# Second attention of a two-layer vision tower: softmax division moved from the probabilities to the values, row sums from ones columns in V

## The chip, the core and the metric

The kernel is one program on one core of a Trainium2 chip. Its time is the device time of one execution in microseconds (us). The core's engines each run their own queue in order: TensorE (PE; its weight loads are listed apart as PEld), VectorE (DVE), ScalarE (ACT), GpSimd (POOL) and SyncE (SP), which here only starts DMAs. They meet at semaphores alone.

## The reference

64 images of 64 tokens, 4096 tokens of width 256 in all. `h` goes through patch embedding, attention, a mixture of experts, a second attention and a second mixture of experts; each of the last four is added to `h` after a layernorm without weights. The second attention, the only part that is changed, has 16 heads of width 16:

```python
cq = gelu(x @ wq + bq);  ckv = gelu(x @ wkv + bkv)          # width 64
q = gelu(concat([cq @ wqc + bqc, rope(x @ wqr + bqr)]))     # 128 + 128
k = gelu(concat([ckv @ wkc + bkc, rope(x @ wkr + bkr)]))
v = ckv @ wv + bv
scores = einsum('bhqd,bhkd->bhqk', q, k) / sqrt(16)         # 64 x 64 per image and head, causal
attn = softmax(scores);  out = einsum('bhqk,bhkd->bhqd', attn, v)
return out @ wo + bo
```

## The kernel before

The stage `attention1_phase` runs over 8 tiles of 512 tokens (8 images), and each tile over 4 chunks of 128 tokens (2 images). Chunk number is g, its tile t, its place in the tile c. n is the next tile. Projections of tile n are made while tile n - 1 is in its attention. All order is written out by hand, in one function `pair` for each engine that lists calls of small helpers; the lists are unrolled in Python. Each helper waits for its inputs by a semaphore and counts another up.

For one chunk the way is: `scores` (TensorE, L2566; two masks as 128x512 products and 16 matmuls of a 32-row head pair, into the PSUM tile p_s, which is single) - `shift` (VectorE, L2403 to L2408: maximum per row, subtraction, into s) - `exp` (ScalarE, L2314, in place in s) - `row_sums` (VectorE, L2410 to L2414: sum per row, reciprocal) - `probabilities` (GpSimd, L2223: s times the inverse sum, 128 x 1024) - `turn_probabilities` (TensorE, L2590: eight 128x128 transposes into p_t) - `turned_out` (ScalarE, L2318: copy to pt) - `values` (TensorE, L2597 to L2605) - `output_high`, `output_low` (ScalarE L2322, VectorE L2416: the attention's output plus the bias of V, split into a rounded part ot_hi and the rest ot_lo) - `output` (TensorE, L2610: ot by wo, six matmuls, into columns 0 to 255 of p_w) - `add` (VectorE, L2424 to L2429: into h).

In `values` the weights are V: vz holds V of 8 head pairs, for each pair 32 columns, with one head's 64 keys in the upper and the other's in the lower partitions and zeros elsewhere. A matmul takes a 128 x 32 block of vz as weights and 64 queries of pt as the moving operand, and its result lands with the features on the partitions: 32 partitions by 64 queries. Four head pairs fill the four column groups of the array. The result is therefore already turned as `output` wants its weights. A 32-bit matmul shows as two records, so a chunk's 16 matmuls are x32 in the rows.

Beside the chunks, tile n needs `turn_rows`, `from_rows` 0 to 4 (the compressed part and the four rope products; each six 512-column matmuls), `from_compressed` (Q and K of the compressed part) and `values_in` 0 to 3 on TensorE, two banks of p_j in turn; `turned_high`, `compressed`, `queries_keys`, `values_out` on ScalarE, which also loads a table whenever it changes between gelu and exp; `turned_low`, `compressed_low`, `rotate` 0 to 3, `normalised`, `statistics` on VectorE; `rope_add` and `add_bias` on GpSimd. In tiles 0 and 1 GpSimd also gathers the last rows of the expert stage before (`late_gather`), and VectorE works them in, in `late_pieces`, in tile 2 (rows) and tile 3 (their statistics).

## Time and profile before

| | us |
|---|---|
| median of 3 runs (lowest, highest) | 1619.34 (1617.81, 1620.17) |
| span of the profiled execution, the only time the page gives for it | 1622.5 |
| PE busy in it, PEld busy | 1393.5 (86%), 1221.3 (75%) |
| DVE, ACT, POOL busy | 1051.8 (65%), 755.3 (47%), 643.1 (40%) |
| mean granted TensorE clock, of full speed | 0.927 |
| the second attention, from its first matmul to its last addition into h | 884.0 to 1189.7 |

A row of the windows view below gives for each engine its busy time and, in brackets, its number of instructions, then the TensorE clock granted, the DMA engines' busy share and the rate. A row of a timeline is: start, duration, engine, line, operation, output<-inputs, shape, count; brackets at its end hold the idle time of the engine ahead of it and what ended it. A matmul's duration includes its way through the array, so a row of many, one behind the other, ends later than the next group starts.

### The profile page before, as it was taken

The numbers are of one execution on the slowest core, as the hardware profiler recorded it, in microseconds if no ns is written. First come the engines' busy times: TensorE is split into PE (matmuls) and PEld (weight loads), VectorE is DVE, ScalarE is ACT, GpSimd is POOL, SyncE is SP. The second block draws the span as 40 slices with busy tenths as digits, with TensorE's granted clock in tenths as the row PEclk, the third lists the DMA queues.
The fourth block names the chain that finished last, engine by engine and source line by source line (L and its number), as shares of the span: only waits on it lengthen the run. The fifth ranks groups of instructions, "written<-read, shape, count | busy, mean of one in ns | idle before, by whom it ended". The sixth has DMA issues, their size and how long they took to land. (4 is left out here: it accounts for less than half of the span.)

```text
span 1622.5 us, 37180 instructions
## 1 busy us (share of the span) xinstructions
PE 1393.5 (86%) x14188; PEld 1221.3 (75%) x14188; DVE 1051.8 (65%) x2196; ACT 755.3 (47%) x1288; POOL 643.1 (40%) x720
## 2 busy tenths in 40 slices
PE   6979999999999986888881888899866999989983
PEld 5867878888888875888880566666666889989983
DVE  4754565575475487766665468988758857466754
ACT  5424444444444443244550567777632355645520
POOL 4015312102102004465445255343364565663665
PEclk9999999999999997889995899999956999999997
DMA  7314655235235005246762000000063377877843
GB/s 281 117 29 169 227 170 180 78 128 174 92 120 183 2 2 208 79 139 217 217 189 65 7 28 21 2 1 2 2 249 121 105 240 242 261 240 240 258 140 91
DMA packets 142884, 215.58 MB, mean 133 GB/s; under 512 B 14336, under 2 KB 112768, under 8 KB 141824
## 3 DMA queue, kind: packets, MB, share of 16 engines
q1 hardware_dynamic: 121648, 160.20, 29.9%
q0 software_dynamic: 18624, 52.45, 10.2%
q8 instruction: 119, 1.95, 0.5%
q10 hardware_dynamic: 2448, 0.61, 0.2%
q14 instruction: 45, 0.37, 0.1%
HBM read 103.64 MB, written 109.58 MB: 131 GB/s over the span
## 5 line engine op out<-in xcount | busy, mean ns | idle before, releaser
L125 PE MATMUL e_p_gu<-e_w_hi,e_xt_hi 128*128 (+1 forms) x676 | 202.4, 299 | 10.0 <-DVE e_xt_lo L723 9.5
L125 PE MATMUL e_p_gu<-e_w_hi,e_xt_lo 128*128 (+1 forms) x676 | 196.5, 291 | 0.0
L125 PE MATMUL e_p_gu<-e_w_lo,e_xt_hi 128*128 (+1 forms) x676 | 196.5, 291 | 0.0
L1273 POOL DMA_INDIRECT e_xn<-results,e_row_of x112 | 115.0, 1027 | 77.8 <-issue 42.4
L125 PEld LDWEIGHTS e_p_gu<-e_w_hi,e_xt_hi 128*128 128x128 f32 x676 | 134.5, 199 | 12.4 <-issue 12.0
L125 PEld LDWEIGHTS e_p_gu<-e_w_lo,e_xt_hi 128*128 128x128 f32 x676 | 134.9, 200 | 0.0
L125 PEld LDWEIGHTS e_p_gu<-e_w_hi,e_xt_lo 128*128 128x128 f32 x676 | 134.9, 199 | 0.0
L125 PE MATMUL e_p_y<-e_w_hi,e_hid_hi 128*128 (+1 forms) x338 | 112.6, 333 | 9.0 <-DVE e_hid_lo L742 7.0
L1254 POOL DMA_INDIRECT rows<-e_xn,e_row_of x96 | 94.2, 981 | 60.1 <-issue 41.8
L1940 DVE TENSOR_TENSOR a_ot_lo<-a_O,a_ot_hi 128x1024 fp32r<-128x1024 f32 x32 | 39.1, 1223 | 114.6 <-ACT a_ot_hi L1883 114.6
L125 PE MATMUL a_J<-a_xt_hi,w_qk_hi 128*128 128x512 f32 x256 | 106.9, 418 | 7.4 <-DVE a_xt_lo L1958 5.4
L2223 POOL TENSOR_TENSOR a_s<-a_s,a_total 128x1024 f32<-128x1024 f32 x32 | 60.9, 1904 | 118.2 <-DVE a_total L2414 117.5
L1299 ACT ACTIVATE e_gated<-e_p_gu 128x256 f32<-128x256 f32 x112 | 43.2, 385 | 126.0 <-PE e_p_gu L125 105.1
L125 PE MATMUL a_J<-a_xt_lo,w_qk_hi 128*128 128x512 f32 x256 | 101.3, 396 | 0.0
L125 PE MATMUL a_J<-a_xt_hi,w_qk_lo 128*128 128x512 f32 x256 | 101.3, 396 | 0.0
L125 PE MATMUL e_p_y<-e_w_lo,e_hid_hi 128*128 (+1 forms) x338 | 97.5, 288 | 0.0
L125 PE MATMUL e_p_y<-e_w_hi,e_hid_lo 128*128 (+1 forms) x338 | 97.3, 288 | 0.0
L1357 DVE TENSOR_TENSOR e_xt_lo<-e_p_xt,e_xt_hi 128x512 fp32r<-128x512 f32 x98 | 67.5, 689 | 23.5 <-ACT e_xt_hi L1292 15.5
L1292 ACT CAST e_xt_hi<-e_p_xt 128x512 fp32r<-128x512 f32 x98 | 57.5, 586 | 53.3 <-PE e_p_xt L1592 49.2
L1524 DVE SCALAR_TENSOR_TENSOR h<-e_xn,e_weight,h 128x256 f32<-128x256 f32 x112 | 54.2, 484 | 40.3 <-DMA e_xn<-results,e_row_of 37.3
L125 PE MATMUL a_J<-a_w_hi,a_ot_hi 128*128 128x256 f32 x256 | 73.5, 287 | 7.7 <-DVE a_ot_lo L1940 7.7
L1837 POOL CAST w_qk_in<-w_qk_in 128x768 fp32r<-128x768 f32 x24 | 21.9, 913 | 146.5 <-DMA w_qk_in<-in_we 146.5
(335 smaller groups left out, 4383.0 us busy)
## 6 DMA issues: line engine op xcount, KB each, us to landing
e_moved<-rows SPq DMA_DIRECT2D x121, 256.0 KB
results<-e_y SPq DMA_DIRECT2D x121, 256.0 KB
rows<-a_zero SPq DMA_DIRECT2D x28, 1024.0 KB, 5.8
pa_x<-in_x SPq DMA_DIRECT2D x7, 1536.0 KB, 6.4
w_qk_in<-in_we SPq DMA_DIRECT2D x24, 384.0 KB, 6.3
we_parts<-w_qk_in SPq DMA_DIRECT2D x24, 384.0 KB, 2.3
we_parts<-a_e_lo SPq DMA_DIRECT2D x24, 384.0 KB, 2.4
e_w_hi<-we_parts SPq DMA_DIRECT2D x4, 1536.0 KB, 16.1
```

Of the source, the lines that this page charges most:

```text
L125: mm = eng.matmul(out, lhs[a], rhs[b], start=start and n == 0, stop=stop and n == len(terms) - 1, skip_group_check=skip)
L1254: pool.indirect_dma_start(out=d["rows"][c][0:rooms[c] * P], out_offset=bass.IndirectOffsetOnAxis(ap=row_of[:, n, k:k + 1], axis=0), in_=ow ...
L1273: pool.indirect_dma_start(out=yg[g % RING][:, k, :], out_offset=None, in_=d["results"][c][0:rooms[c] * P], in_offset=bass.IndirectOffsetOn ...
L1292: act.copy(xt[0][i % 2][:], p_xt[i % 2][:]).then_inc(xt_hi, 1)
L1299: act.activation(gated[h % 2][:], p_gu[h % 2][:].rearrange("p (b n) -> p b n", n=2 * INNER)[:, :, 0:INNER], ACT.Silu)\
L1357: dve.tensor_tensor(xt[1][i % 2][:], p_xt[i % 2][:], xt[0][i % 2][:].bitcast(F32), ALU.subtract).then_inc(xt_lo, 1)
L1524: last = dve.scalar_tensor_tensor(row, yg[g % RING][:, k, :], weight[:, n, k:k + 1], row, ALU.mult, ALU.add)
L1837: pool.tensor_copy(e_hi, e_in).then_inc(e_split, 1)
L1940: dve.tensor_tensor(ot[1][:], p_o[:].rearrange("p i (j q) -> p j i q", q=SEQ), ot[0][:].bitcast(F32), ALU.subtract)\
L2223: pool.tensor_tensor(row_groups(s[c]), row_groups(s[c]), per_row(totals[c]), ALU.mult).then_inc(p_done, 1)
```

## The change

The probabilities are no longer divided. `exp` is followed by the transposes directly. vz gets two more columns for each head pair (V_COLS = 34), set to one once at the start, each in its head's partitions, so that the values product gives each row's sum beside the values. For that product the operands change places: a 128 x 64 block of pt is the weights, the 34 columns of vz move, and the result has the queries on the partitions: 64 partitions by 34 columns, two images in the two halves of the array. VectorE then takes the reciprocal of the 16 sums per token and multiplies the 256 values by it, out of PSUM into a new tile o (`scale`). TensorE turns o by two 128x128 transposes into the unused columns 256 to 511 of p_w (`turn_outputs`), from where `output_high` and `output_low` read. `row_sums` and `probabilities` go. The order of all four lists is rewritten: a chunk's output steps come later by a part of a slot, `output` now stands behind the scores of its slot, `exp(g + 3)` behind `values_out` 0 and 1, `rotate(n, 3)` behind `output_low(g)`, and `output_high(g + 2)` and `output_low(g + 2)` behind the splitting of the turned rows of tile n + 1.

The diff, blank lines and untouched lines left out where marked:

```diff
--- before.py
+++ after.py
@@ -44,6 +44,7 @@
...
+V_COLS = 2 * DK1 + 2
...
@@ -2165,10 +2166,11 @@
...
-        vz = [sb(f"vz{i}", [P, IMG_T, PAIRS, 2 * DK1]) for i in range(2)]
+        vz = [sb(f"vz{i}", [P, IMG_T, PAIRS, V_COLS]) for i in range(2)]
...
-        mx, totals = sb("mx", [P, 2 * PAIRS]), [sb(f"total{i}", [P, 2 * PAIRS]) for i in range(CH)]
+        mx, inv = sb("mx", [P, 2 * PAIRS]), sb("inv", [P, PAIRS, 2])
...
+        o = sb("o", [P, PAIRS, 2, DK1])
...
@@ -2184,10 +2186,13 @@
...
-        row_tile, max_done, s_out, exp_done, summed, inverse, p_done = (
-            sem(n) for n in ("row_tile", "max", "s_out", "exp", "summed", "inverse", "p_done"))
+        row_tile, max_done, s_out, exp_done, inverse, scaled, o_turned = (
+            sem(n) for n in ("row_tile", "max", "s_out", "exp", "inverse", "scaled", "o_turned"))
...
+
+        sums_and_values = p_o[:, 0:PAIRS * V_COLS].rearrange("p (j f) -> p j f", f=V_COLS)
+        p_ot = p_w[:, D:2 * D]
...
@@ -2207,6 +2212,11 @@
...
+            pool.wait_ge(zeros, 1)
+            for i, part in enumerate(vz):
+                for head in range(2):
+                    pool.memset(part[SEQ * head:SEQ * (head + 1), :, :, 2 * DK1 + head:2 * DK1 + head + 1], 1.0).then_inc(zeros, 1)
+                    pool.wait_ge(zeros, 2 + 2 * i + head)
...
             def add_bias(t):
@@ -2217,11 +2227,6 @@
...
-            def probabilities(g, c):
-
-                pool.wait_ge(inverse, g + 1)
-                pool.tensor_tensor(row_groups(s[c]), row_groups(s[c]), per_row(totals[c]), ALU.mult).then_inc(p_done, 1)
-
             def rope_add(n, i, place):
...
@@ -2237,10 +2242,8 @@
             def pair(t2, last=False):
...
-                    g = CH * t
...
-                    probabilities(g + 1, 1)
...
@@ -2249,22 +2252,16 @@
                         rope_add(t + 1, 2, K_SWAP)
...
-                    probabilities(g + 2, 2)
-                    if few is not None:
...
-                    probabilities(g + 3, 3)
-                    if few is not None:
...
-                        probabilities(g + 4, 0)
...
-            probabilities(0, 0)
...
@@ -2321,10 +2318,10 @@
             def output_high(g):
-                act.wait_ge(o_mm, g + 1)
+                act.wait_ge(o_turned, g + 1)
...
-                    done = act.activation(ot[0][:, b], p_o[:, b * P:(b + 1) * P], ACT.Identity, bias=bias[:, 7 + b:8 + b])
+                    done = act.activation(ot[0][:, b], p_ot[:, b * P:(b + 1) * P], ACT.Identity, bias=bias[:, 7 + b:8 + b])
...
             def pair(t2, last=False):
@@ -2333,31 +2330,32 @@
...
                     turned_out(g)
+                    if not is_first(t):
+                        output_high(g - 1)
...
+                    exp(g + 2, 2)
+
+                    turned_out(g + 1)
...
-                    exp(g + 2, 2)
-
-                    turned_out(g + 1)
...
                         queries_keys(n, 1 - u)
+
+                    turned_out(g + 2)
...
-
-                    exp(g + 3, 3)
...
                         values_out(n, 1 - u, range(0, 2))
-                    turned_out(g + 2)
+                    exp(g + 3, 3)
...
                         values_out(n, 1 - u, range(2, 4))
                         exp(g + 4, 0)
...
-                    output_high(g + 2)
-
+
+                    turned_out(g + 3)
...
                         turned_high(n + 1)
-                    turned_out(g + 3)
-                    output_high(g + 3)
+                    output_high(g + 2)
...
                         exp(g + 5, 1)
...
@@ -2368,7 +2366,7 @@
...
             queries_keys(0, 0)
-            act.wait_ge(zeros, 1)
+            act.wait_ge(zeros, 5)
             values_out(0, 0, range(4))
             exp(0, 0)
             turned_high(1)
@@ -2376,6 +2374,7 @@
...
+            output_high(CH * TILES - 1)
...
         def _(dve):
@@ -2407,16 +2406,20 @@
...
-            def row_sums(g, c):
-                dve.wait_ge(exp_done, g + 1)
-                dve.tensor_reduce(totals[c][:], row_groups(s[c]), AX.X, ALU.add).then_inc(summed, 1)
-                dve.wait_ge(summed, g + 1)
-                dve.reciprocal(totals[c][:], totals[c][:]).then_inc(inverse, 1)
+            def scale(g):
+
+                dve.wait_ge(o_mm, g + 1)
+                dve.reciprocal(inv[:], sums_and_values[:, :, 2 * DK1:V_COLS]).then_inc(inverse, 1)
+                dve.wait_ge(inverse, g + 1)
+                at_least(dve, o_turned, g)
+                dve.tensor_tensor(o[:], sums_and_values[:, :, 0:2 * DK1].rearrange("p j (h f) -> p j h f", f=DK1),
+                                  inv[:].rearrange("p j (h f) -> p j h f", f=1).broadcast_to([P, PAIRS, 2, DK1]),
+                                  ALU.mult).then_inc(scaled, 1)
             def output_low(g):
...
-                    done = dve.scalar_tensor_tensor(ot[1][:, b], p_o[:, b * P:(b + 1) * P], bias[:, 7 + b:8 + b],
+                    done = dve.scalar_tensor_tensor(ot[1][:, b], p_ot[:, b * P:(b + 1) * P], bias[:, 7 + b:8 + b],
...
@@ -2441,52 +2444,54 @@
...
-                    row_sums(g + 1, 1)
...
-                        add(t - 1, g - 1, 3)
+                        output_low(g - 1)
                     shift(g + 2, 2)
...
                         rotate(n, 0)
-                    output_low(g)
+                    if not is_first(t):
+                        add(t - 1, g - 1, 3)
...
+                    scale(g)
...
                         rotate(n, 1)
                         rotate(n, 2)
+
+                    output_low(g)
+                    if more:
                         rotate(n, 3)
-
-                    row_sums(g + 2, 2)
+                    shift(g + 3, 3)
                     add(t, g, 0)
-                    shift(g + 3, 3)
-                    output_low(g + 1)
+                    scale(g + 1)
...
                         normalised(n + 1)
...
-                    add(t, g + 1, 1)
-                    row_sums(g + 3, 3)
+                    output_low(g + 1)
...
                         shift(g + 4, 0)
+                    add(t, g + 1, 1)
...
+                    scale(g + 2)
...
                         statistics(t - 1)
-                    output_low(g + 2)
...
                         turned_low(n + 1)
+                    output_low(g + 2)
...
-                        row_sums(g + 4, 0)
                         shift(g + 5, 1)
                     add(t, g + 2, 2)
-                    output_low(g + 3)
+                    scale(g + 3)
...
@@ -2521,12 +2526,12 @@
                 rotate(0, i)
             shift(0, 0)
             turned_low(1)
-            row_sums(0, 0)
             shift(1, 1)
...
+            output_low(CH * TILES - 1)
...
@@ -2588,7 +2593,7 @@
...
             def turn_probabilities(g, c):
-                pe.wait_ge(p_done, g + 1)
+                pe.wait_ge(exp_done, g + 1)
...
@@ -2598,14 +2603,24 @@
...
+                at_least(pe, scaled, g)
...
-                    for i in range(2):
-                        for q in range(4):
-                            mm = pe.matmul(p_o[32 * q:32 * q + 32, b * P + i * SEQ:b * P + (i + 1) * SEQ],
-                                           vz[u][:, 2 * c + i, 4 * b + q, :], pt[:, scored(b, q), i * SEQ:(i + 1) * SEQ],
+                    for q in range(4):
+                        for i in range(2):
+                            mm = pe.matmul(p_o[SEQ * i:SEQ * (i + 1), (4 * b + q) * V_COLS:(4 * b + q + 1) * V_COLS],
+                                           pt[:, scored(b, q), i * SEQ:(i + 1) * SEQ], vz[u][:, 2 * c + i, 4 * b + q, :],
...
+
+            def turn_outputs(g):
+
+                pe.wait_ge(scaled, g + 1)
+                at_least(pe, ot_lo, g)
+                rows = o[:].rearrange("p j h f -> p (j h f)")
+                for b in range(KD):
+                    mm = pe.transpose(p_ot[:, b * P:(b + 1) * P], rows[:, b * P:(b + 1) * P], core.ident[:])
+                mm.then_inc(o_turned, 1)
             def output(g):
...
@@ -2622,35 +2637,41 @@
...
                     turn_probabilities(g, 0)
...
-                        output(g - 1)
+                        turn_outputs(g - 1)
                     scores(t, u, g + 2, 2)
...
                         from_rows(n, 1)
+                    if not is_first(t):
+                        output(g - 1)
                     values(t, u, g, 0)
...
                         from_rows(n, 2)
                         from_rows(n, 3)
                     turn_probabilities(g + 1, 1)
-                    output(g)
+                    turn_outputs(g)
...
                         from_rows(n, 4)
...
                     scores(t, u, g + 3, 3)
+                    output(g)
                     values(t, u, g + 1, 1)
                     turn_probabilities(g + 2, 2)
...
                         values_in(n, range(0, 2))
+                    turn_outputs(g + 1)
+                    if more:
+                        scores(n, 1 - u, g + 4, 0)
                     output(g + 1)
...
-                        scores(n, 1 - u, g + 4, 0)
                         values_in(n, range(2, 4))
                     values(t, u, g + 2, 2)
                     turn_probabilities(g + 3, 3)
...
+                    turn_outputs(g + 2)
...
                         scores(n, 1 - u, g + 5, 1)
                     output(g + 2)
@@ -2669,6 +2690,7 @@
             from_rows(1, 0)
...
+            turn_outputs(CH * TILES - 1)
             output(CH * TILES - 1)
```

## Rows read from the trace of the kernel before

**Rows 1.** Windows view, one row per tile: engine busy, count, clock.

```profile
918.10:956.70 38.60, 35.15 (x383) 26.34 (x383) 24.28 (x35) 25.06 (x37) 20.76 (x16) 0.83 0.10 29
956.70:993.20 36.50, 31.02 (x390) 23.28 (x389) 29.37 (x48) 24.85 (x37) 20.72 (x16) 1.00 0.10 30
...
1028.80:1064.40 35.60, 29.85 (x385) 22.46 (x385) 32.06 (x71) 24.59 (x37) 12.50 (x7) 1.00 0.01 2
...
1096.70:1129.10 32.40, 30.55 (x390) 23.03 (x390) 26.91 (x48) 24.90 (x38) 12.56 (x8) 1.00 0.01 2
1129.10:1160.00 30.90, 29.00 (x379) 21.58 (x377) 24.38 (x43) 23.34 (x35) 12.51 (x8) 1.00 0.01 2
1160.00:1190.00 30.00, 20.44 (x270) 15.74 (x258) 19.72 (x43) 11.42 (x19) 7.58 (x5) 0.73 0.01 1
```

**Rows 2.** Who waited for GpSimd's multiplication L2223: us in total, times.

```profile
  PE a_T L2593: 19.9, 17
```

**Rows 3.** Groups by line, 985 to 1154 us: busy us, mean ns, idle before.

```profile
L2223 POOL TENSOR_TENSOR a_s<-a_s,a_total 128x1024 f32<-128x1024 f32 x21 | 40.0, 1904 | 72.9 <-DVE a_total L2414 72.3
...
L2412 DVE TENSOR_REDUCE a_total<-a_s 128x16 f32<-128x1024 f32 x20 | 24.3, 1213 | 1.6 <-ACT a_s L2316 1.3
...
L2429 DVE TENSOR_TENSOR h<-h,a_W 128x256 f32<-128x256 f32 x20 | 7.7, 387 | 1.2 <-PE a_W L125 1.1
...
L2414 DVE RECIPROCAL a_total<-a_total 128x16 f32<-128x16 f32 x20 | 5.1, 253 | 0.7
```

**Rows 4.** Timeline of TensorE's weight loads in tile 5.

```profile
1101.30 0.44 PEld L2586 LDWEIGHTS a_S<-a_kz,a_qt 32*64 32x64 f32 x16 [0.42 <-issue]
...
1104.29 0.49 PEld L2605 LDWEIGHTS a_O<-a_pt,a_vz 128*32 128x32 f32 x32 [0.36 <-issue]
```

**Rows 5.** Timeline of TensorE's matmuls in tile 5.

```profile
1101.30 1.46 PE L2586 MATMUL a_S<-a_kz,a_qt 32*64 32x128 f32 x32
...
1104.29 0.65 PE L2605 MATMUL a_O<-a_pt,a_vz 128*32 128x64 f32 x32
...
1107.74 1.03 PE L2593 MATMUL a_T<-ident,a_s 128*128 128x128 f32 x8
...
1111.72 0.50 PE L125 MATMUL a_J<-a_comp_hi,w_attention_hi 128*128 128x512 f32 x1 [0.17 <-DVE a_rope L2397]
...
1118.13 0.36 PE L125 MATMUL a_W<-w_attention_hi,a_ot_hi 128*128 128x256 f32 x1 [0.28 <-DVE a_ot_lo L2419]
...
1118.92 0.60 PE L2578 MATMUL a_S<-mask_bf,ident_bf 128*128 128x512 bf16 x2
...
1123.30 1.09 PE L2593 MATMUL a_T<-ident,a_s 128*128 128x128 f32 x8 [0.17 <-POOL a_s L2223]
...
1127.02 0.38 PE L125 MATMUL a_W<-w_attention_hi,a_ot_hi 128*128 128x256 f32 x1
```

**Rows 6.** Timeline of ScalarE in tile 5.

```profile
1108.81 1.01 ACT L2320 COPY a_pt<-a_T 128x1024 f32<-128x1024 f32 x1 [0.80 <-PE a_T L2593]
...
1117.36 1.28 ACT L2316 ACT_TABLE_LOAD   x1
1118.66 1.06 ACT L2316 ACTIVATE a_s<-a_s 128x1024 f32<-128x1024 f32 x1
1119.62 1.50 ACT L2310 COPY a_vz<-a_J 64x256 f32<-64x256 f32 x4
...
1124.71 0.63 ACT L2327 ACTIVATE a_ot_hi<-a_O,a_bias 128x128 fp32r<-128x128 f32 x2
1125.30 1.01 ACT L2278 CAST a_xt_hi<-a_J 128x1024 fp32r<-128x1024 f32 x1
```

**Rows 7.** Timeline of VectorE in tile 5.

```profile
1110.91 0.75 DVE L2397 SCALAR_TENSOR_TENSOR a_rope<-a_J,a_bias,a_sin 128x512 f32<-128x512 f32 x1 [1.98 <-PE a_J L125]
...
1125.51 0.60 DVE L2419 SCALAR_TENSOR_TENSOR a_ot_lo<-a_O,a_bias,a_ot_hi 128x128 fp32r<-128x128 f32 x2
1126.34 1.23 DVE L2385 TENSOR_TENSOR a_xt_lo<-a_J,a_xt_hi 128x1024 fp32r<-128x1024 f32 x1 [0.23 <-ACT a_xt_hi L2278]
```

2 lines of the change are left out of this document (1 added, 1 removed).

## The prediction

> **What bounds the kernel now.** Only the second attention is changed, so I read first the windows of that stage, one for each tile of 512 tokens [rows 1]. Tiles run 30.9 to 38.6 us. In tile 5 (1096.7 to 1129.1) TensorE is busy 30.55 us of 32.40, VectorE 26.91, ScalarE 24.90, GpSimd 12.56: TensorE is the bound with under 2 us left. In tile 3 (1028.8) TensorE does 29.85 of 35.60 and VectorE 32.06: it carries late pieces there (in tile 2 the rows of the combine before, in tile 3 their statistics), and both engines wait in turn. Two tiles have no row of their own: tile 2 lasts the 35.6 us of tile 3, tile 4 the 32.3 of tile 5. Then who stops TensorE: the GpSimd multiplication by the inverse sums. The transposes of the probabilities waited for it 19.9 us in 17 places [rows 2], which is nearly all of what TensorE loses. Last, the engines' order inside a tile [rows 4 to 7]: there one sees which work lies between a chunk's steps, and that has to be redone for the new order.
>
> **What the change removes.** Per chunk (32 of them): a VectorE sum of 1.21 us and a reciprocal of 0.25, and the GpSimd multiplication of 1.90 [rows 3]. The way from the exponential to the transposes gets 3.4 us shorter, so all 19.9 us of those waits should go: exp(g+1) is finished long before its transposes in every slot. From VectorE's load comes back the new reciprocal (same size, 0.25, taken from PSUM) and the multiplication of 128x256 out of PSUM, for which the nearest row is the addition of the same size, 0.39 us [rows 3]. VectorE gets 1.46 - 0.64 = 0.8 us less per chunk, 3.3 per tile. Nothing of that is on TensorE's path in tiles 4 and 5.
>
> **What it adds on TensorE.** First two transposes per chunk. Eight take 1.03 us with their tail [rows 5], so two are bounded by a quarter of it, 0.26, and by half, 0.5, since a group has a fill and a tail however short it is; I take 0.3, nearer to the first, because the next group starts before the tail is out. Second, the values product. Now its 32 weight loads are 32 columns wide, in four column groups, and take 0.49 us, the group 0.65 [rows 4, 5]. New, the probabilities are the weights: 64 columns each, in two groups, with 34 columns moving in place of 64. Bound below: as now, 0.65. Bound above: the scores' 32 matmuls, with 64 columns loaded and 128 moving, take 1.46 us [rows 5]. Nearest are the scores' loads, also 64 wide: 16 in 0.44 us [rows 4], so 32 in 0.88; doubled width in half the groups makes 0.49 into 0.98. I take 1.05 for the group, +0.4. Sum on TensorE: 0.7 us per chunk, 2.8 per tile, 22 in all. That is already about the 20 us given back.
>
> Two rules weighed beside this. By the Trainium skill, page "TensorE: Matmul & The Clock Gate", section "LDWEIGHTS (loading the stationary operand)", a load takes its columns divided by 1.2 GHz: 27 ns for 32 columns, 53 for 64. In a row of 32 this would be 0.85 us now; the trace has 0.49, so loads of different column groups overlap here, and the doubling stands. By the page "TensorEngine Tiling (Array Packing)", section "Instruction Overhead", a matmul with few moving columns is no shorter than one with about 60: going from 64 to 34 would give nothing back; no row of before shows a moving operand that narrow.
>
> **Where new waits come.** I wrote the new order of all four queues out with the rows' durations. Two places give way.
> (a) Last slot, TensorE's output(g+2). In the old order ot_hi of that chunk came ahead of ScalarE's xt_hi, and ot_lo ahead of xt_lo. Now, from the moment that turn_outputs(g+1) is done, ScalarE does one after another ot_hi 0.63, V copies 1.50, the table load 1.28, exp 1.06, V copies 1.50, exp 1.06, pt 1.01, xt_hi 1.01 [rows 6] = 9.05; then VectorE xt_lo 1.23 and ot_lo 0.60 [rows 7], together 10.9, with pick-ups 11.1. TensorE has between the same points: from the scores at 1118.92 to output at 1127.02 8.10 us, plus output(g+1) 0.79 (1118.13 to 1118.92), which moved in there, plus 0.7 of new work, less 0.17 old idle [rows 5] = 9.4. Wait: 1.7 us. Queued behind it are values(g+3) and the next tile's first product, so it is on the path.
> (b) rotate 3 of the rope now stands behind output_low(g) on VectorE, which waits for ot_hi(g), which ScalarE makes after pt(g+1). From the transposes at 1107.74: pt is done 2.1 us later (1108.81 + 1.01), then ot_hi 0.63, ot_lo 0.60, rotate 0.75, 4.1 in all. TensorE was ready for the K product, which needs that bank, at 1111.55 (1111.72 less its 0.17 of idle): 3.8 us, less the output product of 0.79 that moved behind it, plus 0.3 of turn_outputs = 3.3. Wait 0.8 to 0.9 in place of the 0.17 of now [rows 5 to 7].
> The other new waits (scaled(g+1) ahead of turn_outputs) have cover: VectorE has the product's end and 0.9 us of its own, TensorE the eight transposes and, in every slot but the last, projections. add(g) now stands ahead of scale(g+1), but output(g) precedes values(g+1) on TensorE, so nothing is turned round.
>
> Edits at nothing: the four memsets of ones fall in the stage's opening, where GpSimd then waits for constants and for the rope anyway; the gathers of the late rows, no longer between multiplications, start sooner and are needed in tile 2 only; SP's queue is not touched. If the cover of the memsets were gone they would cost under 0.5 us once.
>
> **Sum.** A whole tile in the new order: 30.55 + 2.8 + 2.6 = 36.0 if every wait is added; written out queue by queue the order closes at 35.5, since busy time in the windows counts the tails of groups that a wait then covers. I take 35.5 (estimate from rows 1 and 5 to 7). Against now: tile 1 36.5 to 35.5, -1.0; tiles 2 and 3 have VectorE's late pieces, which stand in front of ot_lo in (a) (1.2 us more each): 36.7 against 35.6, +1.1 and +1.0; tiles 4 and 5 +3.1 each; tile 6 has no next-next tile to turn, so (a) is 0.9: +1.1. Tile 0 wins its first waits for GpSimd, a part of the 19.9, and pays (a) and (b): 0. The last tile is a chain, chunk by chunk: 1.21 + 0.25 + 1.90 = 3.4 us out and 0.25 + 0.39 + 0.3 of transposes, 0.4 of product and their pick-ups in, but its outputs wait for one another through ScalarE as in (a), and part of it ran at the lower clock [rows 1]: a gain of 1 us at most, taken as 0. Sum +8.4 us. The profiled execution spans 1622.5 us, 3.2 above the median of the runs (1619.3) and 2.3 above the highest of them, so a profile of the new kernel would be near 1631 and the median 1619.3 + 8.4 = 1627.7. Stages behind this one start at a barrier and take the shift whole.
>
> **The rivals.**
> 1. Faster: no new stall. If ScalarE's queue in (a) is ahead of my order by 1.5 us, because copies start sooner than I drew them, and the values product stays at 0.65 to 0.75, each tile is what TensorE needs: 30.55 + 4 x 0.3 = 31.8. Tile 1 gains 4.7, tiles 2 and 3 3.8 each, 4 and 5 0.5 each: -13, so 1606 to 1609. It decides at a stall under about 0.5 us per tile. For it speaks that VectorE and GpSimd lose load and that 19.9 us are real. Against it the ScalarE chain, whose every step is a row [rows 6]. Chance 0.22.
> 2. Even: product at 0.7 in place of 1.05, 1.4 us per tile, of which (a) takes 0.3 back; with seven tiles 7.7 less: 1620. Chance 0.16.
> 3. Loads and streams of the values product in series: 1.4 us (near the upper bound above), +0.35 on 32 chunks = 11, of which (a) hides a quarter: +8.4, 1636. Against it: the loads of now overlap, 32 of them in 0.49 us [rows 4]. Chance 0.13. (By the Trainium skill's rule above, loads in a row would make 32 x 53 ns = 1.7 us of it and some 1642 of the time.)
> 4. Clock. In the last stretch the granted clock is 0.73 and in tile 0 0.83 while tiles 1 to 6 hold 1.00 [rows 1]; 1.7 us of wait per tile, beside 0.9, could let it fall to 1.2 GHz within each tile. Tile 3 is idle for 5.75 us of its 35.6 and keeps 1.00, which speaks against. Tile 0 is the price: 38.6 at 0.83 against 35.5 is 3 us; in six tiles 18: 1645. Chance 0.09.
> Forecast itself 0.40.
>
> **How the numbers follow.** A measurement of this kernel tells about 0.2% (3.2 us). Faster by more: rival 1 and little else, 0.23. Within: rival 2 and the near edge of the forecast, 0.17. Slower: 0.60. The likeliest case has 1622 to 1634 for itself; the range goes to 1607, the faster rival, and to 1640, past rival 3, and leaves the clock case out.
>
> **What would show it.** Right: in tiles 4 and 5, 35 to 36 us each; TensorE waiting for ot_lo over 1 us once a tile; no wait of a_T for GpSimd; the values group about 1.0 us. Wrong: a tile of under 32.4 us there, a_W waiting nowhere over 0.5 us, or a values group of 0.65. Tile 1 should be faster in every case but the last two.

## The result, and the profile after

| | before | changed |
|---|---|---|
| median us (lowest, highest), 4 runs each | 1618.57 (1616.62, 1620.17) | 1643.22 (1637.72, 1648.49) |
| ratio, with its 95% interval | | 1.0134 (1.0104 to 1.0164) |
| profiled execution: span, and its own time | 1622.5 | 1646.7, 1648.49 |
| mean granted TensorE clock in it | 0.927 | 0.921 |
| PE, DVE, ACT, POOL busy | 1393.5, 1051.8, 755.3, 643.1 | 1416.7, 1026.0, 761.6, 581.5 |
| second attention, its first matmul to the next stage's first | 306.1 | 330.9 |

The changed kernel is 1.3% slower. The prediction said slower, by 8 us; it is 24.6 by the medians and 24.8 in the stage, so the loss is all in the stage that was changed, and the time lies outside the range. The busy times hold what the change moves: VectorE and GpSimd have 26 and 62 us less, TensorE 23 us more, by records that include what a lower clock adds.

The windows of the changed kernel, one row per tile as in [rows 1], cut in both kernels at the first transpose of a tile's chunk 0; columns: window, length, each engine's busy time and instructions, granted TensorE clock of full speed, DMA share, GB/s. First row: the opening, ahead of tile 0; last row: tile 7.

```profile
886.10:920.90 34.80, 24.62 (x150) 18.35 (x151) 17.23 (x16) 14.12 (x21) 11.82 (x11) 0.79 0.06 14
920.90:958.00 37.10, 34.12 (x386) 27.20 (x389) 21.84 (x36) 25.32 (x36) 13.05 (x11) 0.92 0.10 30
958.00:993.00 35.00, 32.29 (x393) 26.11 (x396) 23.97 (x47) 24.90 (x37) 11.03 (x9) 1.00 0.09 24
993.00:1031.60 38.60, 35.05 (x394) 28.18 (x397) 30.01 (x63) 24.90 (x37) 4.90 (x3) 0.93 0.01 1
1031.60:1071.60 40.00, 36.61 (x394) 29.77 (x397) 27.87 (x66) 26.40 (x39) 4.90 (x3) 0.88 0.01 1
1071.60:1110.20 38.60, 35.88 (x394) 29.13 (x397) 24.35 (x48) 24.90 (x37) 4.88 (x3) 0.90 0.01 1
1110.20:1148.50 38.30, 35.58 (x394) 28.88 (x397) 24.05 (x47) 24.90 (x37) 4.88 (x3) 0.90 0.01 2
1148.50:1181.50 33.00, 30.86 (x380) 25.02 (x382) 20.95 (x40) 23.42 (x36) 4.88 (x3) 0.97 0.01 1
1181.50:1217.00 35.50, 27.88 (x268) 22.97 (x269) 16.64 (x44) 10.95 (x19) 0.04 (x1) 0.60 0.00 1
```

For the comparison, the last tile of before in the same cut:

```profile
1161.90:1190.00 28.10, 20.29 (x258) 15.74 (x258) 17.85 (x42) 10.79 (x17) 5.71 (x4) 0.71 0.01 1
```

In that cut the tiles of before are 36.1 (opening), 38.5, 36.5, 35.6, 35.7, 32.3, 32.3, 30.9, 28.1. The changed kernel's, from the opening on, differ by -1.3, -1.4, -1.5, +3.0, +4.3, +6.3, +6.0, +2.1, +7.4: 24.9 us. Two things are to be seen. Tiles 4 and 5 were to take 35 to 36 us and take 38.6 and 38.3, with TensorE busy 35.9 and 35.6 of that. So they aren't idle; their matmuls last longer, and the clock column says why: 0.88 to 0.93 in tiles 2 to 5, where [rows 1] have 1.00, and 0.60 in the last tile against 0.71.

Whom TensorE waits for in this stage (engine, tile and line, then who ended it: us in total, times, longest):

```profile
PE a_W L126 <- DVE a_ot_lo L2422: 17.7, 12, 2.2
...
PE a_J L126 <- DVE a_rope L2396: 4.6, 10, 0.8
```

All 19.9 us of [rows 2] are gone, as drawn. In their place stand 17.7 for ot_lo (7.3 before) and 4.6 for the rope (2.9 before). With 0.8 for pt before and 1.4 for the scaled o after, these waits fell from 30.9 us to 23.7, and the stage lost 25: the length of the waits by itself can't be the reason.

Tile 4 of the changed kernel on TensorE (start, duration, engine, line, operation, tiles, shape, count; in brackets the idle time ahead and what ended it):

```profile
1085.81 0.51 PE L126 MATMUL a_J<-a_comp_hi,w_attention_hi 128*128 128x512 f32 x1 [0.63 <-DVE a_rope L2396]
...
1097.37 1.13 PE L2611 MATMUL a_O<-a_vz,a_pt 128*64 128x34 f32 x32
...
1100.32 0.38 PE L2622 MATMUL a_W<-ident,a_o 128*128 128x128 f32 x2
...
1104.23 0.36 PE L126 MATMUL a_W<-w_attention_hi,a_ot_hi 128*128 128x256 f32 x1 [1.70 <-DVE a_ot_lo L2422]
...
1105.24 0.41 PE L126 MATMUL a_W<-w_attention_hi,a_ot_lo 128*128 128x256 f32 x1
1105.59 1.93 PE L2611 MATMUL a_O<-a_vz,a_pt 128*64 128x34 f32 x32
1107.45 0.79 PE L126 MATMUL a_J<-a_xt_hi,w_attention_hi 128*128 128x512 f32 x1
```

The wait ahead of output(g+2), (a) of the prediction, is 1.70 us, where 1.7 was drawn. The rows around it have the rest of the loss. Ahead of it a values product takes 1.13 us; behind it the very same 32 matmuls take 1.93, the output product's matmuls go from 0.28 to 0.41, and the projections of 512 columns from 0.39 and 0.50 to 0.63 and 0.79. That is the engine at the lower of its two levels, 1.2 GHz in place of 2.4. It stays so until 1112, some 7 us. The other waits for ot_lo have the same behind them: 2.20 us at 1025.67, then half speed to 1033; 1.10 at 1056.28, for 3.4 us; 0.97 at 1066.10, to 1074; 1.70 at 1142.33, to 1149; 1.12 at 1178.73, to 1193; and in the last tile 1.46, 1.94 and 1.55, with half speed from 1200 to its end. Behind 1.70 at 953.03 it lasts 3.4 us, and behind 1.70 at 989.60 there is none. That last one ends tile 1, which holds 1.00 and lasts 35.0 us: the change with its wait but without the fall, half a microsecond under the forecast's whole tile.

By the windows, (1 - clock) times twice the length is the time at half speed: 81 us in this stage against 44 before (14.6 + 5.9 + 0 + 5.4 + 9.6 + 7.7 + 7.7 + 2.0 + 28.4 for the rows above). 37 us more at half speed are at most 18.5 us of delay. With it the loss reads up to 18.5 for the clock and 6 or more for what the prediction had in its sum.

### The profile page after: what moved, and what is told of

It is laid out like the page before. It is cut to its first block and busy times, and to the rows that moved or that the text cites. A ratio compares the mean times of both kernels' runs of the same rounds, so it can differ in the third digit from the quotient of the medians.

```text
span 1646.7 us, 37296 instructions
## 1 busy us (share of the span) xinstructions
PE 1416.7 (86%) x14221; PEld 1253.0 (76%) x14252; DVE 1026.0 (62%) x2196; ACT 761.6 (46%) x1288; POOL 581.5 (35%) x692
## 5 line engine op out<-in xcount | busy, mean ns | idle before, releaser
L1255 POOL DMA_INDIRECT rows<-e_xn,e_row_of x96 | 94.6, 985 | 57.3 <-POOL router_bias L1249 35.7
L2233 POOL TENSOR_TENSOR a_rope<-a_rope 128x512 f32<-128x512 f32 x16 | 20.5, 1281 | 214.5 <-DVE a_rope L2396 214.5
L126 PEld LDWEIGHTS e_p_y<-e_w_hi,e_hid_hi 128*128 128x128 f32 x338 | 66.2, 196 | 10.6 <-DVE e_hid_lo L743 7.1
```

The lines of the kernel that those rows point to most:

```text
L126: mm = eng.matmul(out, lhs[a], rhs[b], start=start and n == 0, stop=stop and n == len(terms) - 1, skip_group_check=skip)
L1255: pool.indirect_dma_start(out=d["rows"][c][0:rooms[c] * P], out_offset=bass.IndirectOffsetOnAxis(ap=row_of[:, n, k:k + 1], axis=0), in_=ow ...
L2233: pool.tensor_tensor(rope[i][:], rope[i][:], rope[i + 1][:], ALU.add).then_inc(rope_sum, 1)
```

## The experiments

Two theories stood after that. The clock theory (C in the expectations): the work and the waits that the change adds are worth what the forecast says, about 8 us, and the other 17 come from the clock, which falls behind wait (a). Its rival (W): the waits and the added work take all of it themselves, through the order of the queues, and the clock is only a companion. In the kernels below that carry added products, these read constants and write to free columns that nobody reads afterwards; nothing of the computation is left out. The kernel before was run again beside each group of experiments, median 1621.91 us (31 runs) for e1 to e4, 1620.89 (29) for e5 to e8, 1622.18 (22) for e9 and e10; each ratio is to those. The kernel before ran from 1613 to 1632 in them, wider than in the first four runs, so ratios and their intervals are compared, not times across groups.

### The wait shortened by order: e1_splits_first

The ScalarE chain of (a) has xt_hi 1.02 ahead of ot_hi and, on VectorE, xt_lo 1.22 ahead of ot_lo. Both are put behind, as in the kernel before:

```diff
                     turned_out(g + 3)
+                    output_high(g + 2)
                     if not last:
                         turned_high(n + 1)
-                    output_high(g + 2)
...
+                    output_low(g + 2)
                     if not last:
                         turned_low(n + 1)
-                    output_low(g + 2)
```

> The changed kernel with one thing turned back: in a tile's last slot ScalarE makes ot_hi(g+2) ahead of xt_hi, and VectorE ot_lo(g+2) ahead of xt_lo, as in the kernel before. This takes away wait (a) of the prediction (1.70 us in a whole tile of the changed kernel) and leaves all added TensorE work. Theory C (the wait is what lets the clock fall: after each of these waits the records run at half speed for some 7 us): the half-speed stretches inside tiles 2 to 6 go too, and the kernel gains 1.7 us for the wait and some 3.5 us for the clock in each of five or six tiles, so 1643 becomes about 1618 to 1623, granted clock 1.00 in the tiles. Rival W (the clock falls for the stage's mixture of work, whatever the waits): the wait alone goes, 6 x 1.7 = 10 us, 1633, and half-speed stretches stay in the tiles.

Measured: 1624.37 us (1618.01 to 1628.64), 1.0019 (0.9992 to 1.0046). Tiles 1, 2, 5 and the last:

```profile
954.40:988.40 34.00, 32.51 (x393) 26.09 (x396) 24.09 (x48) 24.77 (x37) 11.04 (x9) 1.00 0.09 25
988.40:1025.40 37.00, 34.27 (x394) 27.51 (x397) 30.32 (x65) 25.81 (x38) 4.90 (x3) 0.95 0.01 2
1094.20:1128.20 34.00, 32.50 (x393) 26.08 (x396) 24.12 (x48) 24.77 (x37) 4.88 (x3) 1.00 0.01 1
1160.70:1189.20 28.50, 20.33 (x270) 16.00 (x268) 17.02 (x46) 11.12 (x19) 0.01 (x1) 0.87 0.00 1
```

Two swapped pairs take nearly all of the loss back, 1.0134 to 1.0019; the median is 1.4 us above the 1618 to 1623 that theory C gave and 9 below W's 1633. Where the wait is gone the tile holds 1.00 and lasts 34.0. In tile 2 a wait of 1.06 us is left ahead of the same output product (late pieces on VectorE), and behind it the values product takes 1.88 us and the clock of the tile is 0.95: 37.0. This kernel alone doesn't tell C from W, since it removes wait and fall together.

### The wait kept, but filled: e2_filled_wait

Here the order of the changed kernel is left as it is, and so is ot_lo's time. TensorE is given something to do while it waits:

```diff
                         scores(n, 1 - u, g + 5, 1)
+                    if not last:
+                        for _ in range(12):
+                            pe.matmul(p_o[:, 272:512], core.ident_bf[:], core.mask_bf[:, 0:240], start=True, stop=True)
                     output(g + 2)
```

> The changed kernel with its wait (a) kept but filled: ahead of output(g+2) TensorE does twelve 128x240 bf16 products of the mask into columns of the values' bank that nobody reads, 1.2 us of the 1.7, in each tile that turns rows. The chain over ScalarE and VectorE is untouched, so a tile's dependencies are as long as before. Theory C: TensorE is never idle for long, the clock stays at 1.00 within the tiles, and the time falls by the clock's share alone, 3.5 us in five or six tiles: 1623 to 1628. Rival W: no change, 1643, or a little slower.

Measured: 1625.56 us (1620.33 to 1631.51), 1.0024 (1.0004 to 1.0043). The wait of tile 4, with the twelve products ahead of it:

```profile
1096.31 1.40 PE L2679 MATMUL a_O<-mask_bf,ident_bf 128*128 128x240 bf16 x12
1098.08 0.36 PE L126 MATMUL a_W<-w_attention_hi,a_ot_hi 128*128 128x256 f32 x1 [0.36 <-DVE a_ot_lo L2422]
```

Tiles 1, 2, 5 and the last:

```profile
959.40:994.40 35.00, 33.62 (x405) 27.20 (x408) 23.95 (x47) 24.89 (x37) 11.02 (x9) 1.00 0.09 24
994.40:1030.40 36.00, 33.82 (x405) 27.25 (x408) 28.52 (x60) 24.89 (x37) 4.90 (x3) 1.00 0.01 2
1101.50:1136.50 35.00, 33.63 (x405) 27.22 (x408) 23.96 (x47) 24.89 (x37) 4.88 (x3) 1.00 0.01 1
1168.50:1200.00 31.50, 23.53 (x270) 18.90 (x269) 17.11 (x46) 11.12 (x19) 0.03 (x1) 0.73 0.00 1
```

This is what decides. Nothing of the real work got shorter, TensorE got more to do, and the kernel is 1.1% faster than the changed one: 17.7 us by the medians. The clock is 1.00 in tiles 1 to 6, and their lengths are 35.0, 36.0, 36.1, 35.0, 35.0 and 32.0: against before -1.5, +0.4, +0.4, +2.7, +2.7, +1.1, which is the forecast's tile list (-1.0, +1.1, +1.0, +3.1, +3.1, +1.1) within 0.7 us each. Tile 1 lasts the 35.0 us that it had in the changed kernel, where it held 1.00 too: the fillers themselves changed nothing in it. W fell. The last tile has no filler and keeps 0.73, +3.4 against before.

### The added work alone: e3_before_more_pe

The kernel before, with TensorE made busier by 0.87 us per chunk (eight products of 256 columns) ahead of each values product, 28 us of work in all. The change has 0.92 per chunk by its profile (the values product from 0.58 to 1.06 and turn_outputs 0.44, start to start), where the forecast had 0.7. No wait is added.

```diff
                 hold(pe, pt_out, g + 1)
+                for _ in range(8):
+                    pe.matmul(p_o[:, 0:256], core.ident_bf[:], core.mask_bf[:, 0:256], start=True, stop=True)
                 for b in range(KD):
```

> The kernel before with TensorE work added and nothing else: eight 128x256 bf16 products of the mask ahead of each values product, 0.87 us per chunk, what the changed kernel added there by its profile (values 0.58 to 1.06, turn_outputs 0.44 from start to start). Their result is overwritten. If the added work is the larger part of the loss (28 us of work, minus what old idle time hides, 6 us in tiles 1 to 3): 1618 becomes 1636 to 1642 and the clock stays. If added work costs less because TensorE waited anyway: below 1630.

Measured: 1623.7 us (1620.34 to 1628.38), 1.0019 (1.0001 to 1.0037). Tile 0, tile 4, and the last:

```profile
918.00:953.70 35.70, 33.40 (x410) 25.80 (x414) 24.27 (x35) 24.94 (x37) 20.69 (x15) 0.97 0.11 31
1063.00:1097.00 34.00, 33.21 (x417) 25.67 (x420) 27.20 (x49) 26.33 (x39) 12.51 (x7) 1.00 0.01 2
1162.90:1188.50 25.60, 18.52 (x288) 14.16 (x291) 17.72 (x42) 11.25 (x19) 5.74 (x4) 1.00 0.00 1
```

Of the two cases of the expectation the second came, work that costs little (below 1630), and not 1636 to 1642: 3 us by the ratio. In tiles 4 and 5, with under 2 us of idle time in them, 3.5 us of work cost 1.7. In tile 0 and in the last tile the filled time brought more than it cost: the clock goes from 0.85 to 0.97 and from 0.71 to 1.00, and the tiles from 38.5 to 35.7 and 28.1 to 25.6. TensorE waited 8.5 us for GpSimd in place of 19.9. The 3 us are therefore a sum: what the work costs (0.4 to 1.7 us in each of tiles 1 to 6, all at 1.00), less what the clock gives back, since the half-speed time of the stage falls from 44 us to about 20, at most 12 us of gain. This profile is the quickest of its ten executions. The prediction's "22 in all. That is already about the 20 us given back" set work against waits at full price.

### The order alone, in the old kernel: e4_before_late_splits

The kernel before, with only the order of the last slot taken from the change: xt_hi ahead of ot_hi, xt_lo ahead of ot_lo.

```diff
-                    output_high(g + 2)
-
                     if not last:
                         turned_high(n + 1)
+                    output_high(g + 2)
...
-                    output_low(g + 2)
                     if t >= 2:
                         next(late_pieces, None)
...
                     if not last:
                         turned_low(n + 1)
+                    output_low(g + 2)
```

> The kernel before with only the order of the last slot changed as in the changed kernel: ScalarE makes xt_hi ahead of ot_hi(g+2), VectorE xt_lo ahead of ot_lo(g+2). Theory C: a wait of 0.5 to 1 us per tile comes in front of output(g+2), 3 to 6 us in all, and where it is long enough the clock falls for 7 us: 1622 to 1635, with half-speed stretches inside tiles that had none. Rival W: the wait alone, 1621 to 1624, clock 1.00 in tiles 1 to 6.

Measured: 1625.77 us (1624.22 to 1631.07), 1.0022 (1.0005 to 1.0039). Tiles 1, 2, 3 and 5:

```profile
959.70:998.60 38.90, 33.08 (x386) 26.11 (x389) 29.98 (x48) 25.20 (x38) 20.70 (x15) 0.88 0.10 28
998.60:1036.30 37.70, 33.05 (x385) 25.52 (x388) 31.78 (x62) 24.85 (x37) 12.51 (x7) 0.91 0.01 2
1036.30:1073.50 37.20, 32.26 (x385) 24.64 (x387) 30.36 (x65) 23.79 (x36) 12.52 (x7) 0.94 0.01 2
1106.40:1140.40 34.00, 31.63 (x385) 24.31 (x390) 27.95 (x51) 25.57 (x38) 12.52 (x7) 0.95 0.01 1
```

And the wait of tile 1 on TensorE, with a row from behind it:

```profile
993.31 0.55 PE L125 MATMUL a_W<-w_attention_hi,a_ot_hi 128*128 128x256 f32 x1 [2.72 <-DVE a_ot_lo L2418]
...
994.08 0.41 PE L125 MATMUL a_W<-w_attention_hi,a_ot_hi 128*128 128x256 f32 x1
```

The wait for ot_lo is 2.72 us in tile 1, 1.88 in tile 2 (at 1031.03, also followed by a row of 0.55), 0.69 in tile 3 and 1.14 in tiles 4 and 5. The first row behind the wait has 0.55 and a later one 0.41 where [rows 5] have 0.36 for the first; half speed lasts to 1000 behind the one and to 1037.5 behind the other, and of the two of 1.14 us the one in tile 5 has 3.4 us behind it and the one in tile 4 none. So a wait in this place drops the clock without anything of the change. Not all of the lower clock in tiles 1 and 3 is of this kind: 3.4 us of it in each stand behind waits for GpSimd of 2.43 us (at 978.06) and 2.07 (at 1064.09). The loss is only 3.6 us by the ratio, and that time alone would fit both theories; only the trace tells. The profiled execution, 1630.93 us, is the second slowest of the ten, so the usual one may have fewer falls than these rows. In this kernel there is no extra TensorE work, and the transposes that follow wait for GpSimd anyway; that part of the slow stretch falls on idle time would explain the small sum, and wasn't tested by itself.

### The changed kernel again: e8_changed_again

The changed kernel unaltered, on the chip on which e5 to e7 ran.

> The changed kernel as it is, so that the others of this call stand beside it on the same chip. Both theories: 1.2 to 1.6% over the kernel before, half-speed stretches after most of the waits for ot_lo in the last slots.

Measured: 1646.72 us (1634.67 to 1658.14, 6 runs), 1.0132 (1.0097 to 1.0166). The ratio repeats. The tiles of its profile differ: tile 1 lasts 38.6 at 0.90 here and 35.0 at 1.00 in the first, tile 5 38.1. In this execution, the slowest of its six, every wait for ot_lo of 0.96 us and more in tiles 0 to 6 has half speed behind it, also the one of 1.70 at the end of tile 1. So which waits are followed by a fall isn't the same from one execution to the next; the run times spread over 23 us, those of the filled kernel over 11.

### The other wait: e5_rotate_first

e1, and on top rotate 3 back ahead of output_low(g), which should take away wait (b):

```diff
                         rotate(n, 2)
+                        rotate(n, 3)

                     output_low(g)
-                    if more:
-                        rotate(n, 3)
```

> The kernel with the splits of chunk g+2 first (as in e1) and, besides, rotate(n, 3) ahead of output_low(g) on VectorE, which is wait (b) of the prediction undone: 0.63 us in each of seven tiles in the profiles of the changed kernel and of e1. If (b) is on the path: tiles of 33.4 us where e1 had 34.0, 3 to 4 us in all. If something else is late right behind it (ot_lo(g), then output(g)): tiles stay at 34.0 and the time at e1's, 1.002 of before.

Measured: 1623.53 us (1618.69 to 1625.86), 1.0006 (0.9989 to 1.0023). Tile 4 and the last:

```profile
1060.70:1094.30 33.60, 32.87 (x393) 26.06 (x396) 23.84 (x49) 26.26 (x39) 4.90 (x3) 1.00 0.01 2
1159.90:1191.40 31.50, 23.54 (x271) 18.91 (x269) 17.15 (x47) 11.12 (x19) 0.07 (x1) 0.74 0.00 1
```

The waits for a_rope in the stage fall from 4.3 us (e1) to 1.4, and tiles 4 and 5 from 34.0 to 33.6, expected 33.4: 0.4 for a wait of 0.63. In all, 3 to 4 us were expected; the ratios of e1 and e5 differ by 2, with intervals that overlap. The last tile is at 0.74, 31.5 us against 28.5 at 0.87 in e1, though nothing in it was edited; the two profiles differ there by the clock alone. Against the changed kernel on the same chip, 1646.72, the orders undone together are worth 23 us, of the 26 that it is above the kernel before there.

### Fillers where the clock fell: e6_repaired_filled and e7_before_filled

e6 is e5 with fillers where its trace still had the lower clock: in the opening, in tile 6 and in the last tile, whose outputs wait for one another. e7 gives the kernel before the same opening and its own last tile's fillers.

```diff
+            def fill(out, count):
+                n = out.shape[-1]
+                for _ in range(count):
+                    pe.matmul(out, core.ident_bf[:], core.mask_bf[:, 0:n], start=True, stop=True)
...
+                    if not more:
+                        fill(p_j[:, 0, :], 6)
                     output(g + 1)
...
+                    if not more:
+                        fill(p_j[:, 0, :], 9)
+                    elif last:
+                        fill(p_o[:, 272:512], 8)
                     output(g + 2)
...
             turn_rows(0)
+            fill(p_o[:], 8)
...
             from_compressed(0)
+            fill(p_o[:], 12)
             values_in(0, range(4))
             scores(0, 0, 0, 0)
             turn_rows(1)
+            fill(p_o[:], 6)
             scores(0, 0, 1, 1)
+            fill(p_o[:], 5)
...
+            fill(p_j[:, 0, :], 3)
             turn_outputs(CH * TILES - 1)
+            fill(p_j[:, 0, :], 7)
             output(CH * TILES - 1)
```

e7 has the four fills of the opening, 4 more ahead of the first transposes, and in the last tile 2 ahead of the transposes of g+2, 3 ahead of output(g+1), 12 ahead of the transposes of g+3 and 7 ahead of the last output.

> e5 plus fillers: mask products in bf16 of 512 or 240 columns that nobody reads, put where TensorE stands idle in the stage's opening (8, 12, 6 and 5 of them), in the slot before the last tile and in the last tile (8, 6, 9, 3, 7). Theory C: the clock stays at full speed in tile 0 and up to the end of the stage, which had 14 half-speed us in e1 beyond the opening; 3 to 7 us less than e5 and the runs scatter less: 0.995 to 0.998 of before. Rival: fillers only cost their own time where they outlast a wait, 0 to 3 us more than e5.

> The kernel before with the same fillers in the opening (and 4 ahead of the first transposes) and 2, 3, 12 and 7 of them ahead of the waits of its last tile: the control for e6. Theory C: its 27 half-speed us in tile 0 and the last tile fall to under 10, 5 to 9 us less: 0.994 to 0.997 of before. The difference of e6 to this one is then the change's own worth with the clock held in both: more TensorE work, 1.1 us per tile in tiles 4 and 5, less waiting in tiles 1 to 3; about even.

e6 measured: 1616.07 us (1609.93 to 1620.03), 0.9963 (0.9946 to 0.998). Tile 2 and the last:

```profile
986.80:1023.70 36.90, 34.28 (x394) 27.42 (x397) 30.29 (x65) 25.84 (x38) 4.90 (x3) 0.95 0.01 2
1157.80:1184.80 27.00, 23.94 (x292) 16.84 (x293) 17.02 (x46) 11.13 (x19) 0.00 (x0) 1.00 0.01 1
```

e7 measured: 1620.88 us (1616.24 to 1624.98), 0.9995 (0.9978 to 1.0012). Tiles 1, 3 and the last:

```profile
955.30:993.90 38.60, 33.70 (x385) 26.57 (x390) 29.28 (x48) 24.95 (x37) 20.68 (x15) 0.87 0.10 29
1029.40:1067.60 38.20, 33.25 (x384) 24.66 (x388) 32.39 (x71) 24.79 (x37) 12.52 (x7) 0.91 0.01 2
1163.20:1190.90 27.70, 23.36 (x278) 16.54 (x283) 17.90 (x43) 10.79 (x17) 5.76 (x4) 0.82 0.00 1
```

e6 is the first kernel that is faster than before. The last tile goes from 31.5 at 0.74 (e5) to 27.0 at 1.00 with 25 more products in it, whose rows have 5.4 us together. Tile 2 still has its fall, 36.9 at 0.95. The runs were to scatter less than e5's and did not: 10 us against 7. e7 missed: 0.994 to 0.997 was expected of it. The opening and the last tile did gain, but tiles 1 and 3, untouched by the fillers, fell to 0.87 and 0.91: tile 1 behind a wait for GpSimd of 2.44 us (1.22 in the profile of before) and one for ot_lo of 1.53, tile 3 behind one for GpSimd of 1.72. In the profile of before, waits of 1.63 for ot_lo and 1.74 for GpSimd in the same places went by at 1.00. So the step from e7 to e6 isn't a clean price of the change with the clock held; that price stays open.

### How long the wait must be: e9_part_filled

e2 with six fillers in place of twelve, so that a part of (a) is left:

```diff
+                    if not last:
+                        for _ in range(6):
+                            pe.matmul(p_o[:, 272:512], core.ident_bf[:], core.mask_bf[:, 0:240], start=True, stop=True)
                     output(g + 2)
```

> The dose: as e2, but six fillers of 240 columns in place of twelve, so that of the 1.70 us of wait (a) some 1.1 is left. If any wait of over 1 us lets the clock fall: half-speed stretches in the tiles nearly as in the changed kernel, 1.009 to 1.013 of before. If what counts is how long TensorE stands in one go and 1.1 us is short enough (the kernel before has waits of 1.2 to 2.1 us in tiles 1 to 3, mostly without a fall): as e2, 1.001 to 1.004.

Measured: 1633.06 us (1625.76 to 1638.87), 1.0057 (1.0033 to 1.0081); its profiled execution took 1630.81. Tiles 3 and 5, and the wait that is left in tile 4:

```profile
1028.90:1066.80 37.90, 35.48 (x403) 28.61 (x402) 28.03 (x67) 24.96 (x38) 4.90 (x3) 0.94 0.01 2
1101.90:1137.00 35.10, 33.33 (x404) 26.67 (x403) 23.95 (x47) 24.90 (x37) 4.88 (x3) 1.00 0.01 1
```

```profile
1098.45 0.36 PE L126 MATMUL a_W<-w_attention_hi,a_ot_hi 128*128 128x256 f32 x1 [0.98 <-DVE a_ot_lo L2422]
```

The time is between the two expectations. 1.70 us of wait: 1.0132 and 1.0134; 0.98 left: 1.0057; under 0.4 left in tiles 1, 4 and 5 (e2): 1.0024. In the profile, of the fifth quickest of twelve executions, 0.98 us went by at 1.00 in tiles 1, 4 and 5, while tile 3, behind 1.47 at the end of tile 2 and with 1.08 of its own, fell to 0.94. The runs are graded with the length of the wait, not cut at one length; the way that fits both is that a wait drops the clock in some executions and some tiles, and the more often the longer it is. The kept traces bear that out as far as they go. Of the waits for ot_lo in tiles 0 to 6, those of 1.70 us (four each in the two profiles of the changed kernel) have half speed behind them in 7 cases of 8, both of 2.2 us too. Those of 0.96 to 1.13 us have it in 6 of 6 cases in these two profiles, and in 3 of 17 in the profiles of e1, e2, e5, e6, e9 and e10, where the waits of 1.70 us are shortened or gone. So the length isn't all of it.

### Fillers in tiles 2 and 3 as well: e10_filled_late_tiles

e6 plus fillers in tiles 2 and 3, one slot ahead, where the late pieces make TensorE wait:

```diff
                     if not more:
                         fill(p_j[:, 0, :], 6)
+                    elif t in (2, 3):
+                        fill(p_o[:, 272:512], 9)
                     output(g + 1)
```

> e6 with nine more fillers of 240 columns ahead of output(g+1) in tiles 2 and 3, where VectorE's late pieces hold ot_lo back by 1.1 us and where e6 still had one half-speed stretch of 3.4 us. If that stretch comes from this wait: 0 to 2 us less than e6, 0.995 to 0.997 of before, and nothing at half speed between the opening and the end of the stage. If not: as e6.

Measured: 1613.89 us (1611.1 to 1623.22), 0.995 (0.9932 to 0.9968). Tiles 0, 2 and the last:

```profile
922.90:956.80 33.90, 31.72 (x390) 25.04 (x389) 21.02 (x33) 24.24 (x35) 13.05 (x11) 1.00 0.12 33
990.30:1026.00 35.70, 33.85 (x407) 26.99 (x406) 28.89 (x61) 24.91 (x38) 4.91 (x3) 1.00 0.01 2
1160.10:1187.20 27.10, 24.25 (x298) 16.88 (x294) 17.05 (x47) 11.12 (x19) 0.06 (x1) 1.00 0.00 1
```

Its profiled execution, 1623.22 us, is the slowest of its twelve; the time above the others isn't in this stage: against e6's profile the stage starts 3.4 us later, is 1.0 shorter and has 4.6 us more behind it. Every tile holds 1.00, and they last 33.9, 33.5, 35.7, 34.9, 33.6, 33.6, 32.0 and 27.1, the stage 297.0 us against 306.1 before. It beats the kernel before by 0.5% and the changed one by 1.8%; from e6 it isn't told apart, their intervals overlap. Its tiles 4 and 5 are still 1.3 us longer than [rows 1]; it wins in the opening, in tiles 0, 1 and 3 and in the last.

## Why the prediction missed

**What held.** The reading of the bound (TensorE, waits for GpSimd of 19.9 us), and that all of them go. The values product: 1.05 was taken, from the width of its weight loads; 1.13 was measured for the group and 1.06 from its start to the next group's, the weight loads 1.01 against 0.49 in [rows 4]. With that rival 3, which needed 1.4, is out, and rival 2, which needed 0.7, too. By the Trainium skill, page "TensorE: Matmul & The Clock Gate", section "LDWEIGHTS (loading the stationary operand)", 32 loads of 64 columns in a row are 1.7 us, as an estimate from its formula. The trace has 1.01 and speaks against, as [rows 4] did. Two rows of the changed kernel's stretch from 985 to 1154 us (group, count, busy us, mean ns, idle before):

```profile
L2611 PE MATMUL a_O<-a_vz,a_pt 128*64 128x34 f32 x546 | 22.6, 243 | 0.0
...
L2415 DVE TENSOR_TENSOR a_o<-a_O,a_inv 128x256 f32<-128x256 f32 x17 | 7.2, 424 | 0.6
```

The multiplication out of PSUM was put at 0.39 us by its size, 0.42 measured; the reciprocal at 0.25, 0.26 measured. Rival 1 fell at (a): ScalarE wasn't ahead of the order drawn. Its queue in tile 4, to be laid beside [rows 6]:

```profile
1095.37 1.28 ACT L2313 ACT_TABLE_LOAD   x1
1096.66 1.06 ACT L2313 ACTIVATE a_s<-a_s 128x1024 f32<-128x1024 f32 x1
...
1100.39 1.01 ACT L2317 COPY a_pt<-a_T 128x1024 f32<-128x1024 f32 x1
1101.30 1.02 ACT L2275 CAST a_xt_hi<-a_J 128x1024 fp32r<-128x1024 f32 x1
1102.20 0.64 ACT L2324 ACTIVATE a_ot_hi<-a_W,a_bias 128x128 fp32r<-128x128 f32 x2
```

The table load takes 1.28, exp 1.06, pt 1.01, xt_hi 1.02, ot_hi 0.64; then on VectorE xt_lo 1.22 from 1102.35 and ot_lo 0.60 from 1103.49: each step is there, in the order and the length of the working, and the wait comes out at 1.70.

**What was off in size.** turn_outputs 0.38, with 0.44 from its start to the next, where 0.3 was taken; wait (b) 0.63, where 0.8 to 0.9 was. A whole tile with the clock held is 35.0 us (e2), 35.5 in the forecast, and the tile list of the forecast is that of e2 within 0.7 us. That its sum came out is in part luck, as said below. What was wrong by more is the last tile, "a gain of 1 us at most, taken as 0": it is +7.4. In e10 the same chain at full clock is 27.1, which is -1.0 against the 28.1 of before at 0.71; so some 8 us of the 35.5 are the clock, which the 1.12 us at the end of tile 6 and the three waits of 1.46 to 1.94 us let fall. (Against e3's last tile, 25.6 at 1.00 without the change, 27.1 is 1.5 more; part of the old tile's time was clock as well.)

**The step that failed** is rival 4, its chance of 0.09 and the range that "leaves the clock case out". Its mechanism and place were right: 1.7 us of wait per tile and a fall to 1.2 GHz within the tile. Its price of 3 us was taken from tile 0 of the old kernel against a tile of the new one, and the total of 1645 (1643.2 measured) is near in part by luck: against e2 the profile has 2.6, 3.9, 3.6, 3.3 and 1.0 us in tiles 2 to 6, 14.4 in place of 18 in six tiles, nothing in tile 1, and 4.0 in the last tile, which the rival did not count. It was set aside by one sentence: "Tile 3 is idle for 5.75 us of its 35.6 and keeps 1.00, which speaks against". That is a sum over a tile, of many short waits, and says nothing on one wait of 1.7 us between two dense stretches. A row that could have spoken was in the same profile, where the last tile follows tile 6, 29.0 us busy of 30.9 at 1.00:

```profile
1161.92 1.09 PE L2593 MATMUL a_T<-ident,a_s 128*128 128x128 f32 x8 [1.77 <-POOL a_s L2223]
...
1164.48 1.08 PE L2578 MATMUL a_S<-mask_bf,ident_bf 128*128 128x512 bf16 x2
```

One wait of 1.77 us, and the masks behind it take 1.08 in place of the 0.60 of [rows 5]; half speed lasts from 1163 to 1170. The trace of before also holds waits of 1.63 and 2.06 us with no fall behind them, so it could not have given certainty; but a case that one row bears out and others speak against belongs inside the range.

**Two errors of size that cancelled.** The forecast's tile has 2.8 us of added work, 0.9 for (b) and 1.7 for (a), 5.4 in all, of which 1.85 of old idle time and 0.5 of cover are taken off: +3.1. Measured, with the clock at 1.00, the terms are 3.7 (0.92 per chunk), 0.6 and 1.7, 6.0 in all, and the tile is +2.7. So the work was put too low, and what hides behind other work too low as well; that the tile list came out is luck in part. By the experiments tiles 4 and 5 last 32.3 us before, 33.6 with the added work and hardly a wait for the rope (e5), 34.0 with wait (b) (e1) and 35.0 with wait (a) as well, filled (e2): 1.3 for 3.7 us of work, 0.4 for (b), 1.0 for (a). e3 has 1.7 for 3.5 us of other work. What covers the rest of the work, and whether a tile is as long as ScalarE's chain and its wait, no run separates.

**What stays open.** What decides whether a wait drops the clock: 1.70 us at 989.60 and those of 1.63 and 2.06 us before had no fall behind them, while 1.06 and 1.12 us had one in some places and none in others. Waits for the rope of 1.70 and 1.69 us in tile 0 of e6 and e10 had none either. And e1 was expected about 5 us ahead of e2; 1.2 was measured, with intervals that overlap. e1's profiled execution, 1620.78 us, is the second quickest of its ten and e2's, 1631.03, the second slowest, so the tiles of 34.0 may be e1's best and not its usual ones. What the change is worth with the clock held in both kernels is open too, since e7 did not hold it.

## What to carry to other kernels

A new wait on a busy TensorE costs up to its length and then what the lower clock makes of the work behind it: here 1.7 us of wait cost 1.0 by themselves, and were in most cases followed by 3.4 to 7 us of matmuls at half speed, 2.6 to 3.9 us more in each of tiles 2 to 5. So when an edit of the order puts a new wait of 1 us or more into a dense stretch, put the fallen clock into the range at least, and look first for an order that keeps the consumer's last step ahead of work that nobody waits for: two swapped pairs were worth 1.1% here. Where no order does it, matmuls into free PSUM columns, put into the wait itself, hold the clock at little cost (1.0024 with them against 1.0019 for the better order); test that on a run, since whether a given wait drops the clock is not to be had from the wait's length.
